# A four-layer graph and expert network on one core: slice tokens from sums of rows, work moved to GpSimd and SyncE, residuals placed beside products

## The reference

```python
x = x + _L0_gnn_ref(_layernorm(x), edge_index, W, b)      # relu(sum over edges of normalized rows @ W, + b)
x = x + _L0_ffn_ref(_layernorm(x)[None], ...)[0]          # shared expert, and 2 of 8 experts
x = x + _L1_gnn_ref(...)                                  # messages with edge_attr, 2-layer MLP, graph norms
x = x + _L1_ffn_ref(...)                                  # 1 of 32 experts
x = x + _L2_gnn_ref(...)                                  # attention over edges
x = x + _L2_ffn_ref(...)                                  # 2 of 16 experts, layer norm
x = x + _L3_gnn_ref(...)                                  # 4-head attention over edges, elu
x = x + _L3_ffn_ref(...)                                  # attention over 64 slices
```

```python
fx_mid = (x @ W_fx + b_fx)                                # nodes x (8 heads x 64)
slice_weights = softmax((x_mid @ W_slice + b_slice) / temp)
slice_norm = slice_weights.sum(axis=2)
slice_token = einsum('bhnc,bhng->bhgc', fx_mid, slice_weights) / (slice_norm[..., None] + 1e-05)
```

## Time and profile before

| what | value |
|---|---|
| median of 3 runs | 5455.45 us (5451.37 to 5457.28) |
| the profiled execution | 5460.66 us |
| its span, first to last instruction | 5458.8 us |
| PE busy | 4354.3 us, 80% |
| DVE busy | 3479.1 us, 64% |
| POOL busy | 3320.4 us, 61% |
| ACT busy | 2303.0 us, 42% |
| mean granted clock of PE | 0.865 of full speed |

### The profile page before, as it was taken

One profiled execution on the slowest core, in us unless ns is written; L12 is line 12 of the kernel. 1 busy time (PEld: TensorE's weight loads), 2 busy tenths in 40 slices (PEclk: granted clock), 3 DMA queues, 4 the chain that ended last, 5 costly groups with the idle time before them and its releaser, 6 DMA issues. The chain is left out here.

```text
span 5458.8 us, 88501 instructions
## 1 busy us (share of the span) xinstructions
PE 4354.3 (80%) x20192; PEld 2868.9 (53%) x20192; DVE 3479.1 (64%) x12190; ACT 2303.0 (42%) x7944; POOL 3320.4 (61%) x3594
## 2 busy tenths in 40 slices
PE   6978777999957777656799968888696688878768
PEld 4533436899823335443455547666594333346536
DVE  8977884411167774545555558887415688878875
ACT  6910552333333334123555545554143455545421
POOL 7777775666467774451577757775124477758710
PEclk8966998999956667677999989999697899999978
DMA  2443336698667773152444458886474488877500
GB/s 69 156 144 104 105 105 204 240 301 290 200 178 206 207 208 73 56 129 78 125 131 129 129 156 287 277 277 186 147 210 123 135 230 232 232 208 230 174 19 24
DMA packets 528344, 916.64 MB, mean 168 GB/s; under 512 B 95861, under 2 KB 378436, under 8 KB 519396
## 3 DMA queue, kind: packets, MB, share of 16 engines
q0 software_dynamic: 154432, 449.76, 29.5%
q1 hardware_dynamic: 330254, 346.48, 20.2%
q10 hardware_dynamic: 43158, 114.74, 6.7%
HBM read 741.02 MB, written 169.60 MB: 167 GB/s over the span
## 5 line engine op out<-in xcount | busy, mean ns | idle before, releaser
L1212 PE MATMUL bank<-small 128*125 128x256 f32 x1660 | 737.3, 557 | 281.6 <-DVE small L1175 169.9
L1156 POOL DMA_INDIRECT small<-tabA,idxD x830 | 800.7, 965 | 263.9 <-issue 150.2
L1212 PEld LDWEIGHTS bank<-small 128*125 128x125 f32 x1660 | 339.5, 252 | 674.0 <-DVE small L1175 372.4
L2649 POOL DMA_INDIRECT big<-tabT,edge x415 | 403.9, 973 | 246.4 <-SPq L200 120.3
L3185 POOL DMA_INDIRECT small<-tabC,idxD x415 | 409.5, 987 | 185.6 <-SPq L200 59.4
L2923 POOL DMA_INDIRECT big<-tabB,idxD x415 | 399.2, 962 | 169.1 <-issue 89.6
L1066 POOL DMA_INDIRECT eaS<-edge,rowE x391 | 393.2, 1006 | 163.5 <-issue 115.2
L1762 DVE COPY small<-bank 128x256 f32<-128x256 f32 x176 | 74.7, 424 | 617.9 <-PE bank L1819 601.3
L1187 DVE TENSOR_TENSOR big<-big,bank 125x256 f32 x830 | 345.5, 416 | 148.1 <-PE bank L1212 131.7
L3263 PE MATMUL bank<-big,cst 128*125 128x512 f32 x830 | 424.7, 593 | 0.7 <-ACT big L3250 0.7
L1717 POOL DMA_INDIRECT small<-tabA,small x176 | 168.0, 955 | 380.8 <-PE bank L1795 186.8
(11 more groups left out here) (531 smaller groups left out, 10802.2 us busy)
## 6 DMA issues: line engine op xcount, KB each, us to landing
big<-in_L_w ACTq DMA_DIRECT2D x56, 1024.0 KB
small<-eaS SPq DMA_DIRECT2D x415, 128.0 KB
eaS<-small SPq DMA_DIRECT2D x415, 128.0 KB, 3.5
big<-eaS SPq DMA_DIRECT2D x415, 128.0 KB, 3.5
edge<-in_ea SPq DMA_DIRECT2D x390, 128.0 KB
big<-in_L2f_w ACTq DMA_DIRECT2D x64, 512.0 KB
big<-rowsD SPq DMA_DIRECT2D x104, 256.0 KB, 4.2
ytab<-small SPq DMA_DIRECT2D x120, 128.0 KB
```

Of the source, the lines that this page charges most:

```text
L1156: g.indirect_dma_start(out=self.gb[k % self.RG], out_offset=None, in_=K.tabA, in_offset=row_index(K.idxD, k)).then_inc(*self.got.up(k))
L1212: p.matmul(self.K.bank[k % 4][0:PT, 0:D], self.oh[k % self.RO][:, 0:PT], self.gb[k % self.RG], start=True, stop=True).then_inc(*self.summe ...
L2649: g.indirect_dma_start(out=self.rows(k)[:, 0, :], out_offset=None, in_=K.tabT, in_offset=row_index(K.idxS, k)).then_inc(*self.got.up(k))
```

## The change

It has seven parts.

1. `L0Out`: scale and bias go from one DVE instruction to two POOL instructions a tile, a multiply by the node's scale and an add of the bias. DVE keeps the other three.
2. `EdgeRows`: the 28 edge rows at L0's end go; every second expert tile issues four instead of three.
3. `L1Mlp`: the layer norm of x and its add go beside the first products; ACT's last pass is cut into five pieces, and PE's way back uses four banks instead of two.
4. `Moe`, the routers of L1 and L2: the stores go from ACT to SP, each split into 112 and 13 rows; the second weights' loads go one stage earlier.
5. `L2Project`: the last two casts of each tile go from ACT to POOL.
6. `Slices`: loads and fold go into the elu stage before. The loop no longer makes values; it sums normalized rows times slice weights in two banks (128 x 512 each) and multiplies by W_fx once, behind the loop. POOL sums the slice weights (`self.weight`), one 125x512 add a tile.
7. More banks and buffers in that loop (`RX` = 7 rows kept).

```diff
@@ class L0Out
+    def gpsimd(self, g, added):
+        g.wait_ge(*self.t_b)
+        g.wait_ge(*added.all)
+        for t in range(T):
+            at = self.acc[0:PT, t * D:(t + 1) * D]
+            g.tensor_scalar(at, at, K.dis[0:PT, t:t + 1], None, ALU.mult).then_inc(*self.spread.up)
+            if t >= 1:
+                self.biased(g, t - 1)
+        self.biased(g, T - 1)
+    def biased(self, g, t):
+        at = self.acc[0:PT, t * D:(t + 1) * D]
+        g.wait_ge(*self.spread.n(t + 1))
+        g.tensor_tensor(at, at, self.K.wb[0:PT, :], ALU.add).then_inc(*self.scaled.up)
...
-                v.scalar_tensor_tensor(out=at, in0=at, scalar=K.dis[0:PT, i:i + 1], in1=K.wb[0:PT, :], op0=ALU.mult, op1=ALU.add).then_inc(*self.scaled.up)
@@ class Moe, scores_sync; store_row goes from scores_scalar
+            store_rows(s, K.tabA[t * PT:(t + 1) * PT, :], self.xn[t % self.RN][0:PT, :], self.x_out.up(t))
@@ expert_gpsimd
-                self.side.edges.gpsimd(g, 1)
+                self.side.edges.gpsimd(g, 1 + k % 2)
@@ class L1Mlp, vector
+                if f == 1:
+                    ln_apply(K, v, t, self.tmp[t % 2][0:PT, :]).then_inc(*self.normed.up)
+                if f == 3:
+                    v.wait_ge(*self.normed.n(t + 1))
+                    v.tensor_tensor(K.xt(t), K.xt(t), self.tmp[t % 2][0:PT, :], ALU.add).then_inc(*self.joined.up)
...
-            ln_apply(K, v, t, tp).then_inc(*own.up)
-            v.wait_ge(*own.all)
-            v.tensor_tensor(K.xt(t), K.xt(t), tp, ALU.add).then_inc(*own.up)
@@ class L2Project
     def gpsimd(self, g):
+        assert self.source.done == EC
         for t in range(T):
+            for m in range(2):
+                g.wait_ge(*self.less[1].n(2 * t + m + 1))
+                g.tensor_copy(self.third(t, m, 2), self.rest(t, m)).then_inc(*self.part[2].up)
...
-            for c, late in ((2, 6), (1, 5), (0, 4)):
+            for c, late in ((1, 5), (0, 4)):
@@ class Slices, gpsimd
+        for t in range(T):
+            g.wait_ge(*self.soft.n(t + 1))
+            sv = self.sw[0:PT, t * 512:(t + 1) * 512]
...
+                g.tensor_tensor(w, w, sv, ALU.add).then_inc(*self.weighed.up)
@@ tensor
-                for q in range(4):
-                    m = p.matmul(K.bank[4 + q][:, 0:129], self.sw[...], self.fx[...], start=(t == 0), stop=(t == T - 1))
+                for c in range(2):
+                    m = p.matmul(K.bank[4 + c][:, :], self.xn[t % self.RX][0:PT, c * 128:(c + 1) * 128],
+                                 self.sw[0:PT, t * 512:(t + 1) * 512], start=(t == 0), stop=(t == T - 1))
...
-                    m = p.matmul(K.bank[3][0:PT, :], xT[:, c, :], self.wf[:, c * 512:(c + 1) * 512], start=(c == 0), stop=(c == 1))
@@ tensor, behind the meeting
+        p.matmul(K.bank[6][0:64, :], K.ones[0:PT, 0:64], self.weight[0:PT, :], start=True, stop=True).then_inc(*self.norm.up)
+        for h in range(8):
+            p.matmul(K.bank[0][0:64, at], self.bf[0:PT, at], self.weight[0:PT, at], start=True, stop=False)
+            for c in range(2):
+                m = p.matmul(K.bank[0][0:64, at], self.wf[...], self.sums[c][:, at], start=False, stop=(c == 1))
@@ vector, behind the meeting
+        v.tensor_scalar(nr, K.bank[6][0:64, :], 1e-5, None, ALU.add).then_inc(*own.up)
+        v.reciprocal(nr, nr).then_inc(*self.inverse.up)
+        v.tensor_tensor(self.tT[0:64, :], K.bank[0][0:64, :], nr, ALU.mult).then_inc(*self.tokens.up)
@@ build
-            edges.gpsimd(g, 28)
+            l0_out.gpsimd(g, l0_sum.added)
@@ build, SP
+            s.wait_ge(*l1_mlp.flipped.all)
+            m1.weights_sync(s, 0)
+            s.wait_ge(*l1_mlp.second.all)
+            m1.weights_sync(s, 1)
```

More of the change, by code:

```diff
@@ L1295, in __init__ @@
         self.logits = K.mark(T)
-        self.x_out = K.ring(self.RN, T)
+        self.x_out = K.ring(self.RN, T, parts=1 if shared else 2)
         if not shared:
@@ L1364, in scores_sync, with weights_sync @@
             s.wait_ge(*self.normed.n(t + 1))
[L1365 to L1371, removed]
+            store_rows(s, K.tabA[t * PT:(t + 1) * PT, :], self.xn[t % self.RN][0:PT, :], self.x_out.up(t))
+        for t in range(T - self.RN, T):
+            s.wait_ge(*self.x_out.n(t))
+    def weights_sync(self, s, i):
+        lo, hi = i * self.step, min((i + 1) * self.step, self.E)
+        s.dma_start(self.w2s[:, lo * self.w2:hi * self.w2].rearrange("p (e c) -> p e c", c=self.w2),
+                    self.K.a[self.key + "w"].rearrange("p (e c) -> p e c", c=self.ecols)[:, lo:hi, self.w2off:]).then_inc(*self.weights.up)
     def scores_gpsimd(self, g):
@@ L2245, in scalar @@
         a.wait_ge(*self.scale2.n(1))
-        for o in range(2):
-            ins = a.activation(self.h2v[:, o, :], self.h2v[:, o, :], ACT.Relu, scale=self.q[2][:, o:o + 1], bias=self.q[3][:, o:o + 1])
-        ins.then_inc(*self.final.up)
+        for c in range(5):
+            at = slice(c * 5 * PT, (c + 1) * 5 * PT)
+            for o in range(2):
+                ins = a.activation(self.h2v[:, o, at], self.h2v[:, o, at], ACT.Relu, scale=self.q[2][:, o:o + 1], bias=self.q[3][:, o:o + 1])
+            ins.then_inc(*self.final.up)
     def vector(self, v):
@@ L3513, in __init__ @@
         self.wq, self.wk, self.wv = W(64), W(64), W(64)
+        self.weight, self.nr = W(512), W(512)
+        self.sums = [W(512) for _ in range(2)]
         self.tickets = [K.ticket() for _ in range(12)]
@@ L3601, in tensor @@
         K.meet(p, "p")
-        p.wait_ge(*self.means.n(1))
-        for q in range(4):
-            m = p.transpose(K.bank[0][0:64, q * 128:(q + 1) * 128], self.tok[:, q * 64:(q + 1) * 64], K.ident)
-        m.then_inc(*self.means_t.up)
+        p.wait_ge(*self.weighed.all)
+        p.matmul(K.bank[6][0:64, :], K.ones[0:PT, 0:64], self.weight[0:PT, :], start=True, stop=True).then_inc(*self.norm.up)
+        p.wait_ge(*self.kept_a.n(1))
+        p.wait_ge(*self.kept_v.n(1))
+        for h in range(8):
+            at = slice(h * 64, (h + 1) * 64)
+            p.matmul(K.bank[0][0:64, at], self.bf[0:PT, at], self.weight[0:PT, at], start=True, stop=False)
+            for c in range(2):
+                m = p.matmul(K.bank[0][0:64, at], self.wf[:, c * 512 + h * 64:c * 512 + h * 64 + 64], self.sums[c][:, at], start=False, stop=(c == 1))
@@ L3692, in vector @@
         self.stats.vector(v)
-        for f in self.fx:
-            ins = v.memset(f.rearrange("p (q c) -> p q c", c=129)[:, :, 128:129], 1.0)
-        ins.then_inc(*self.one.up)
         for i in range(T + 3):
@@ L3925, in _ @@
             K.meet(p, "p")
+            l3_ffn.fold(p)
             K.meet(p, "p")
@@ L3990, in _ @@
             l2_out.sync(s)
+            for i in range(m2.n_w):
+                m2.weights_sync(s, i)
             K.meet(s, "s")
```

131 lines of the change are left out of this document (59 added, 72 removed).

## The result

The changed kernel takes 5401.55 us (median of 4 runs, 5387.83 to 5408.14), the kernel before beside it 5456.36 (5451.37 to 5457.98, 4 runs). The ratio is 0.9898, with a 95% interval of 0.9877 to 0.9918, so it is faster by 1.0%, some 55 us. The profiled execution has a span of 5401.4, 57.4 less than the 5458.8 of before.

A forecast was written before the change was run, and what follows sets the result against it. PE bounded the experts; other stages hung on waits or several engines. Stage terms of +14, 0, -14, -7, -15, 0 and -32 summed to -54, taken off the median 5455.45: 5401 us, range 5372 to 5428.

The forecast's parts named there:

- the projection's balance: L2's projection: two fewer ACT casts gain 18 us, POOL's casts holding DVE up cancel it, 0 in all.
- the upper bound by the line through two shapes: End of L0: POOL's multiply of 256 columns, from its times at 125 and 415 columns, at most 1.03 us.
- DVE's turn: End of L0: POOL and DVE wait for each other at SBUF, adding 0.3 us to each POOL round.
- Rival D: Experts: extra edge-row bytes make DMA the bound, each tile longer by 0.96 us or more, 5465 us; chance 4%.
- the last tile's rest: L1's MLP: work left after POOL's 25 scatters, putting the stage's end at 2261 to 2262.
- rival E: L2's router: early loads land late and stores still meet them, -15 becomes -4, 5412 us; chance 9%.
- the 2 us that the prediction named as a sign: Routers of L1 and L2: no wait of DVE for `tabA` would exceed 2 us.
- The form 3.3 + 2c: L2's projection: round in us, 3.3 plus twice c, DVE's delay by each POOL cast, taken as 0.33; 3.96.
- Rivals A and C: L2's projection: A, casts don't delay DVE, -18, 5383, 20%; C, port costs more, slices too, 5415 to 5422, 12%.
- The fold's part: Slices' start: loads and most of the fold move into the elu stage, leaving 3.8 us before the first tile, -21.3.
- The loop's saving: Slices' loop: one DVE add goes, 0.60 us a round, from 4.86 to 4.26, -15.0 in all.
- the +4.5 of the middle: Behind the slices' loop: at halved clock, last sums cost 1.9 more, small products +2.6 net; +4.5 us.

The follow-up runs named there:

- the last two experiments: Changed kernel with four edge rows in every expert tile: experts' stage 441.45 us; the same with each tile's index scatter moved behind the experts: 420.11 us.

## Why the prediction was right, point by point

The whole came out at 5401.55 for 5401, and that it came so near is luck: the eight stages gave 12.5 more than the sum, and the others took 9 back. Right are the sign and the mechanism of every stage but the projection's balance and the slices' middle.

**End of L0 (+14, measured +14.6).** From POOL's first multiply, 836.01, to the stage's end it is 43.0 us, where the prediction had 42.4. Two errors cancel in it. The multiply was taken at 0.75 and takes 0.91; the upper bound by the line through two shapes, 1.03, was nearer than the 0.75. DVE's turn was charged in every round and costs POOL 0.27 in eleven of 23. The average round of 1.63 is the predicted 1.65 by that accident. The rows bear out the rule of the Trainium skill's "GPSIMD Engine Reference", Specifications, that the two engines contend where DVE has two inputs in SBUF (0.42 against 0.70). The Trainium skill's same page, Engine selection, puts one-input operations on GpSimd at roughly line rate. Beside the 0.41 of DVE's one-input normalization, POOL's casts, 0.40 to 0.59 and 0.53 at the median, come near that; the multiply by a scale per row, 0.91, does not, and was dearer than the add of two tensors (0.63).

**Experts (0, measured -0.4).** Right, with the wrong guard. Rival D watched DMA, whose share rose to the 0.87 that was forecast, and the last two experiments show that at 0.96 PE keeps its pace. The edge was POOL's number of issues: 6.96 us a tile on average in the changed kernel (5.5 issues of 1.265), 7.63 with one more in every second tile. The prediction has POOL's price, 0.6 more a tile, but sets the sum of its issues against nothing, and its 7.5 us a tile is the stage divided by its tiles, where PE's own pace is 7.2.

**L1's MLP (-14, measured -17.5).** The mechanism was right: POOL last, 1.26 apart, DVE 12.5 us early. The size was 3.3 to 3.5 off, in three steps. The prediction added 1.2 for the last tile's rest, which isn't there. It gave the last scatter a whole pitch of 1.26, but the meeting closes 0.14 behind its start. And the first of the 25 starts some 126.4 after the stage's start, by 24 pitches back from the last, where 127.4 was taken. DVE's round was mis-sized as well, 0.86 for the 1.05 taken, which cost nothing here and is why it was so early.

**Routers (-7 and -15, measured -7.4 and -16.0).** Right; of L2's four loads the first was issued at 3769.75 and the last landed at 3795.99, 5.6 us ahead of the router's start, 26 us in all for the 25 taken. DVE's waits for `tabA` in L2 are down to 5.4 us in ten places, none over 1.1, and rival E didn't occur. In L1 they are 7.5 us, and the longest is 2.7, over the 2 us that the prediction named as a sign, at no cost to the stage's forecast. What the prediction's wording missed is that the stores' move would earn part of it by itself, where loads stand beside them.

**L2's projection (0, measured -4.8).** The form 3.3 + 2c holds within 0.05; the term that was mis-sized is c: I took 0.33, it is (1.16 - 0.76) / 2 = 0.20, just under the lower bound that the memset gave (0.22). The round fell from 3.96 to 3.75, 25 x 0.21 = 5.3, and 4.8 of it came; the 1.5 that the prediction saw at the tail for fewer casts did not. Rivals A and C both fall: the port does cost, but little.

**Slices (-32, measured -35).** The fold's part is right: the first normalization stands 4.1 after the stage's start (3.8). The loop's saving is 4.86 - 4.40 = 0.46 a round, not 0.60, which takes 3.5 from the 15: the removed add had covered 0.12 of DVE's wait on its own result. The prediction also read the loop wrongly: it has DVE's instructions follow each other without a gap, before and after, where 0.37 of each round was a wait for ACT in both. The 3.5 is given back at both ends. At the loop's start, before the change, the values' add had to wait for PE:

```profile
5245.19 0.69 DVE L3718 TENSOR_TENSOR small<-bank,big 125x512 f32<-125x512 f32 x1 [1.41 <-PE bank L3593]
```

The third normalization stood 9.20 behind the second there and stands 6.80 behind it now, which is 1.9 more than a round's saving. Behind the loop the clock was granted in full until the small products were done; it fell only with the next ones:

```profile
5312.00:5316.00 4.00, 3.84 (x50) 3.14 (x50) 3.40 (x3) 0.56 (x1) 0.00 (x0) 1.00 0.00 0
...
5319.00:5330.00 11.00, 5.77 (x35) 3.94 (x33) 5.64 (x9) 0.63 (x1) 0.00 (x0) 0.50 0.00 1
```

The prediction had taken it as halved there, as it was before the change from 5368 on. PE had been idle for 3.70 us ahead of its last sums there and for 2.41 here; whether that made the difference no run tells. So the last sums took 1.98 for 1.86 and not 1.9 more, the 24 small products 3.0 instead of 5.7 (5313.02 to 5315.99), and the +4.5 of the middle did not come. The reciprocal that was to be hidden, 3.35 for an estimated 4.0, then became the last to end, 1.3 behind the products. That the errors in this stage nearly cancel is luck.

**Sum.** -54 for -55 of the medians and -57.4 of the spans. The projection, L1's MLP and the slices gave 4.8, 3.5 and 3 more than forecast, the routers 1.4, and stages that nothing touched took 9 back in this one execution. L2's part of that is scatter; for the rest, L1's sums above all, one profile of the kernel before can't tell.

## What to carry to other kernels

Work out an engine's issues per tile against the pace of the engine that sets it, measured in a stretch without head and tail, not against the stage's length over its tiles: here 0.25 us a tile (7.21 less 6.96) was all the room there was, and DMA's share of 0.87 pointed at the wrong resource. Where two engines share a port, the turn costs only on the engine that sets the pace, so a two-input operation may go beside a busy DVE if it runs ahead of it. And before moving work off an engine, look whether its idle time is a chain that another order would break: reordering one instruction in L2's projection and one group in the slices was worth 21 and 11 us, where the projection's stage gained 5 by the move of two casts.

## What was not expected of the hardware

A turn at the shared port is paid by the one or the other: in the same loop POOL's multiply took 0.91 and DVE's relu 0.70 for twelve rounds, then 1.18 and 0.42 for eleven, though in both DVE started 0.05 or 0.06 us behind POOL. What turned it over is open. POOL's multiply of 125x256 by a scale per row (0.91) is dearer than its add of two such tensors (0.63). And TensorE kept its pace with DMA at a share of 0.96, where POOL already waited 23.9 us for loads.
